# The order of TensorE's steps and of two copies in a fused attention with inverse-distance weights

## The reference, cut to what matters

```python
def _shepards_mha(Q, K, V):
    q2 = jnp.sum(Q * Q, axis=-1, keepdims=True)
    k2 = jnp.sum(K * K, axis=-1, keepdims=True)
    sq = q2 + jnp.swapaxes(k2, -1, -2) - 2.0 * jnp.einsum('bhqd,bhkd->bhqk', Q, K)
    dist = jnp.sqrt(jnp.maximum(sq, 0.0))
    W = (SHEP_EPS + dist) ** (-SHEP_P)                     # eps 1e-4, power 2
    W = W / (SHEP_EPS + jnp.sum(W, axis=-1, keepdims=True))
    return jnp.einsum('bhqk,bhkd->bhqd', W, V)

P = jnp.einsum('btd,ed->bte', Xn, W_in) + b_in             # Q, K, V and a gate G
A = _shepards_mha(Q, K, V)
return X + jnp.einsum('btd,ed->bte', G * A, W_out) + b_out
```

## Time and profile before

| | us |
|---|---|
| median of three executions | 3915.79 |
| the profiled execution | 3922.57 |
| its span | 3920.8 |
| PE busy in the span | 3543.4 (90%) |
| DVE busy | 2494.0 (64%) |
| ACT busy | 2228.7 (57%) |
| POOL busy | 646.5 (16%) |

### The profile page before, as it was taken

One profiled execution on the slowest core, in us unless ns is written; L12 is line 12 of the kernel. 1 busy time (PEld: TensorE's weight loads), 2 busy tenths in 40 slices (PEclk: granted clock), 3 DMA queues, 4 the chain that ended last, 5 costly groups with the idle time before them and its releaser, 6 DMA issues.

```text
span 3920.8 us, 56053 instructions
## 1 busy us (share of the span) xinstructions
PE 3543.4 (90%) x22244; PEld 2491.0 (64%) x22244; DVE 2494.0 (64%) x4347; ACT 2228.7 (57%) x2875; POOL 646.5 (16%) x595
## 2 busy tenths in 40 slices
PE   4999999989999999978779779779877999999998
PEld 3555555478888899973323323323326888889998
DVE  4777777553433455547988988988985443335554
ACT  1666666643322344438998998998993332234443
POOL 3333332100122011221300300200000002200212
PEclk7999999899999999988889889889888999999999
DMA  3000000010011134430000000000001001013342
GB/s 123 1 1 1 1 1 1 1 65 6 25 37 32 34 94 115 105 76 8 1 1 1 1 1 1 1 1 1 1 1 65 6 22 38 24 45 91 94 111 40
DMA packets 86664, 124.81 MB, mean 32 GB/s; under 512 B 7752, under 2 KB 73115, under 8 KB 86402
## 3 DMA queue, kind: packets, MB, share of 16 engines
q1 hardware_dynamic: 68738, 100.05, 7.5%
q0 software_dynamic: 17664, 21.17, 3.3%
HBM read 85.02 MB, written 42.55 MB: 33 GB/s over the span
## 4 chain that ended last, share of the span: by engine, by line
PE 32%; ACT 10%; DVE 9%; issue 3%; DVEq 1%; ACTq 0%; POOL 0%; DMA 0%; SPq 0%; POOLq 0%
PE f2ring L1479 14%; PE f2acc L1498 7%; DVE b_w L1831 6%; ACT b_w L1869 5%; PE b_acc L1946 4%; PE b_ring L1958 4%; ACT b_w L1909 4%; ACT L1906 1%; PE b_ring L2008 1%; DVEq L1770 0%; PE b_ring L2006 0%; DVE b_stacks L1747 0%; PE b_ring L1982 0%; PE f2ring L1444 0%; DVE b_w L1775 0%
## 5 line engine op out<-in xcount | busy, mean ns | idle before, releaser
L1831 DVE TENSOR_TENSOR b_w<-b_w 128x2048 f32<-128x2048 f32 x254 | 571.7, 2292 | 25.7 <-ACT b_w L1909 21.7
L1869 ACT ACTIVATE b_w<-b_ring 128x1024 f32<-128x1024 f32 x512 | 485.9, 1037 | 92.2 <-PE b_ring L1958 86.3
L1946 PE MATMUL b_acc<-b_w,b_vg 128*32 128x512 f32 x2048 | 333.0, 740 | 172.6 <-DVE b_w L1831 171.5
L1909 ACT ACTIVATE b_w<-b_w 128x2048 f32<-128x2048 f32 x256 | 468.7, 1897 | 2.1 <-issue 0.4
L1399 ACT ACTIVATE f2hid<-f2ring 128x512 f32<-128x512 f32 (+2 forms) x256 | 132.6, 518 | 577.4 <-PE f2ring L1479 560.4
L1399 ACT ACTIVATE f1hid<-f1ring 128x512 f32<-128x512 f32 (+2 forms) x256 | 132.6, 518 | 576.8 <-PE f1ring L1479 559.8
L1317 DVE TENSOR_TENSOR f1hid<-f1hid,f1ring 128x512 f32<-128x512 f32 (+2 forms) x256 | 150.2, 587 | 439.4 <-ACT f1hid L1399 439.4
L1317 DVE TENSOR_TENSOR f2hid<-f2hid,f2ring 128x512 f32<-128x512 f32 (+2 forms) x256 | 150.2, 587 | 439.3 <-ACT f2hid L1399 439.2
L1958 PE MATMUL b_ring<-b_qT,b_kT 32*128 32x512 f32 x2048 | 411.4, 692 | 18.6 <-ACT b_w L1869 15.0
L1775 DVE TENSOR_SCALAR b_w<-b_w 128x2048 f32<-128x2048 f32 x256 | 305.7, 1225 | 86.7 <-ACT b_w L1869 85.8
L624 ACT ACTIVATE a_prob<-a_wide 128x1024 f32<-128x1024 f32 (+1 forms) x320 | 292.8, 943 | 86.5 <-PE a_wide L730 59.6
(11 more groups left out here) (340 smaller groups left out, 6274.9 us busy)
## 6 DMA issues: line engine op xcount, KB each, us to landing
X<-expert_in SPq DMA_DIRECT2D x16, 650.0 KB, 4.8
expert_in<-a_zeros SPq DMA_DIRECT2D x8, 650.0 KB, 10.1
X<-in_x SPq DMA_DIRECT2D x4, 1024.0 KB, 10.7
x_mid<-X SPq DMA_DIRECT2D x8, 512.0 KB, 3.1
f1raw_x<-in_rd SPq DMA_DIRECT2D x4, 1024.0 KB, 5.3
f1raw_xf<-in_rg SPq DMA_DIRECT2D x4, 1024.0 KB, 5.0
f1raw_xf<-in_ru SPq DMA_DIRECT2D x4, 1024.0 KB, 7.1
f1raw_g<-in_rg SPq DMA_DIRECT2D x4, 1024.0 KB, 4.9
```

The costliest lines, as they stand in the source:

```text
L1831: v.tensor_tensor(one(m), one(m), one(m), ALU.mult).then_inc(s_wts, 1)
L1869: s.activation(w[:, m, 2 * pair:2 * pair + 2, :].rearrange("p h n -> p (h n)"), slot(at + pair), ACT.Ln, scale=SHEP_EPS ** -2).then_inc(R. ...
L1909: s.activation(one(m), one(m), ACT.Sigmoid, scale=-0.5).then_inc(s_sig, 1)
L1946: last = pe.matmul(acc[32 * h:32 * h + 32, qc, :], vg[:, u % 2, h, x, :], w[:, x, h, :], start=(x == 0), stop=(x == TB - 1))
```

## The change

TensorE's list. In the kernel before, between the `values` of period j stood one `dist` tile ahead of m=3, and one each ahead of m=5, 6 and 7; four followed after m=7. Now the tiles 0 and 1 stand back to back ahead of `values` m=3, one each ahead of m=4, 5, 6 and 7, and two follow after m=7. `stack` moves from the start of the odd period to the even period before it: the first stands ahead of `values` m=6, the second at the very end of the period. `project` no longer stands among the `values` m=0 to 2 but between the two `dist` tiles. VectorE's two copies move with their transposes: from after the squares m=0 and 1 of the odd period to after `bound` m=3 (behind `o_rows`) and m=7 of the even one. No instruction is added or removed.

```diff
@@ moved(j)
-        if j % 2 and (j + 1) // 2 < UNITS:
-            out += [("stack", (j + 1) // 2, i) for i in range(SIDES)]
@@ order(j)
+        stacks = [("stack", j // 2 + 1, i) for i in range(SIDES)] if j % 2 == 0 and j // 2 + 1 < UNITS else []
...
         for m in range(TB):
             if m == TB - 5:
-                out += aux + ahead[:1]
-                aux = []
-            elif m > TB - 4:
-                out += ahead[m - TB + 4:m - TB + 5]
-            elif m < TB - 5:
+                out += ahead[:1] + aux + ahead[1:2]
+            elif m > TB - 5:
+                out += ahead[m - 2:m - 1] + (stacks[:1] if m == TB - 2 else [])
+            elif aux and aux[0][0] != "project":
                 out += aux[:1]
                 aux = aux[1:]
             out += [("values", j, m)]
-        return out + ahead[4:]
+        return out + ahead[6:] + stacks[1:]
@@ VectorE, among the squares of period j
-                        elif m < SIDES:
-                            operand(n, m)
@@ VectorE, among the bounds of period j + 1, behind o_rows
+                    if j % 2 == 0 and n < UNITS and m in (3, TB - 1):
+                        operand(n, m // 4)
```

## The result

| | before | changed |
|---|---|---|
| median of four executions, us | 3916.45 | 4033.68 |
| lowest and highest | 3913.46, 3922.16 | 4030.2, 4038.35 |
| span of the profiled execution | 3920.8 | 4028.4 |
| granted clock over the span | 0.941 | 0.923 |

The ratio is 1.0298, with a 95% interval of 1.028 to 1.0316: 117 us slower, where 46 had been forecast and 3985 us was the end of the range. The direction is right. The places are right in part: the phases of p=0, which were to gain 2 us, lose 21. The loss is two and a half times as large.

The account below looks back on a forecast made before the run. ScalarE was taken to bound the second attention. Phase terms +17 (odd), +25 (plain even), +9.5 (p=4), +2.4 (period 30), -2.4 (p=0) and -5.7 (p=1) gave +46 on 3915.8: 3961.6 us, range 3925 to 3985.

Parts of the forecast that it names:

- p=0: Three phases with `project`: 6.39 us idle goes, second tile at T + 2 to T + 6; -2.4 us in all.
- ScalarE bounds the stage and only the logarithm phases can move: Second attention: ScalarE busy 1042.87 of 1136 us; the change can move only the logarithm phases, 556.0 us together.
- the clock's term: TensorE after T: half clock after a long wait makes odd phases 18.6 us instead of 16.4; even ones at full clock.
- Odd phases, the lone pair at half clock after the wait: Twelve odd phases: TensorE waits some 4 us, then runs at 1.2 GHz; 18.6 against 17.2 us, +17 in all.
- p=4: Three phases: half clock plus the stack's transposes and slot wait, 18.6 + 0.95 + 2.1 against 18.5; +9.5 us in all.
- Even phases: Nine plain even phases: full clock, plus stack transposes and slot wait, 19.5 against 16.7 us; +25 in all.
- The slot's chain: Even phases: after `values` 7, `o_rows` and the copy run before tile 6 with nothing beside them, 2.1 us.
- p=1: Three phases, without a stack: 16.9 to 18.9 against 19.5 us; -5.7 us in all.
- Period 30: One phase without a stack, priced at half clock: 18.6 against 16.2 us, +2.4.
- The rival of a full clock: TensorE stays at 2.4 GHz over the wait; odd, p=4 and period 30 phases 2.2 us shorter: +11, 3927; chance 0.14.
- the rival of half clock in even periods: Plain even phases: clock falls again in the wait or has not risen yet; 9 x 2.2 = +20, 3982; chance 0.13.

Follow-up runs that it names:

- e11: The changed kernel with its second distance tile computed whole and needless whole-array filler matmuls in the wait ahead of it (filler not at p=0 and 1): 3991.2 us, ratio 1.0189.
- e3: The kernel before with only `project` moved behind the first distance tile: 3912.3 us, ratio 0.9982.
- e4: The changed kernel with VectorE's copy into `b_qT` put one place ahead of `o_rows`: 3965.9 us, ratio 1.0112.
- e13: e11 with e4's exchange and fillers ahead of `values` 1 and 2 in even periods, `values` 0 in odd ones: 3935.3 us, ratio 1.0043.
- e5: The changed kernel with `project` put back among `values` 0 to 2: 4064.4 us, ratio 1.0377.
- e7: The kernel before with a needless lone pair of distances behind each of `values` 0, 1 and 2 of odd periods: 4009.3 us, ratio 1.0219.
- e12: The changed kernel with its second distance tile waiting until it can be issued whole, no filler: 4015.1 us, ratio 1.0234.
- e9: The kernel before with e3's place of `project` and needless whole-array filler matmuls ahead of `values` 0 to 2: 3900.4 us, ratio 0.9961.

## Why the prediction was right in direction and wrong in size

- *ScalarE bounds the stage and only the logarithm phases can move*: right. They grew by 114.8 us, and what lies between them did not move.
- **The step that failed is the clock's term.** It was mis-sized in the odd phases, put at nothing in the even ones, and at p=0 the place of the second tile behind `project` was forecast too early. The three follow.
- *Odd phases, the lone pair at half clock after the wait*: the mechanism is right, to the hundredth up to T + 4.95; e11 (16.9 without wait and pair) shows that the clock, and not the order, makes these phases long. The term's size is wrong: 18.6, "four more steps of 2.07, less what is still slow in the first (1.44 to the next `values`)", from the single row of p=4. Measured 19.6. Tile 3 starts at T + 8.35 and not at T + 7.4, tile 6 at T + 14.8 and not at T + 13.6, as the half clock holds for all of tile 2 and half of the `values` behind it. That is 12 us of the error.
- *Even phases*: 19.5 forecast, 22.3 measured. The slot's chain is right (1.95 against 2.1). I took the half clock as absent there, a rival at 0.13 and +20, and held that the first pair would end near T and no wait matter. From T + 1 to T + 4 the clock is 0.50 to 0.80 in six of nine, in four of them since it had not risen before T, which is one of the two ways that the rival named. And behind the pause of the slot the 1.2 GHz is back for tile 6 or 7 in 7 of 15, which no case of mine had, though it is the mechanism that I had used for the other end of the phase. Where the clock is full after T the phase is still 20.7; those three are all at p=2, where the phases of the kernel before were longer too (17.1 to 17.8, against 16.4), and what is left of the difference isn't resolved. 25 us; another 5 at p=4, where the same holds (23.4 against 21.65).
- *p=0*: -2.4 forecast, +21 measured. The place of the second tile, "T + 2 to T + 6 (as `project` runs at full or half clock)", was T + 9.5. `project` starts at T - 2.9 and takes 12.4 us at half clock. The trace of the kernel before had a hint: there it runs from 2091.84 to 2102.38, 10.5 us, the most part at half clock, and ScalarE's 6.39 us ahead of T stand behind it. That the clock would be at half through all of it was not to be read there, and what decides it stays open. The place itself is harmless: with `project` at full clock the phase is 18.9 in the old order (e3) and 19.2 in the new (e4, e13), less than the 23.2 of before. It is the second largest miss, 24 us.
- *p=1*: -5.7 forecast, -4.9 measured. Right; e5 shows that the gain belongs to the move of `project` (28.6 without).
- *Period 30*: 18.6 forecast, 19.8 measured, as the odd ones.
- *The rival of a full clock* (3927) is refuted by the 0.50 to 0.60 in 11 of 12 odd phases; *the rival of half clock in even periods* (3982) holds in part, and with the other misses is what carries the time out of the range. The range was too narrow because each of its ends varied one term, while the misses nearly all come from the clock and add up: 12 + 25 + 5 + 1 + 24 + 1 = 68, and 46 + 68 = 114.

## What to carry to other kernels

A TensorE that is waited for should come out of its waits at the full clock: before moving a step, look at the granted clock a few microseconds before and behind each wait, not only at the durations, and price a new pause with the slower matmuls behind it (here 1.9 us of pause cost up to 1.9 more). A matmul pair that used half of the rows cost as much time as a whole tile, and with such pairs in between the clock did not rise (e7), so issue all groups together where the ring has room. Waiting for room alone brought 19 us of the 117 (e12), with work in the wait 43 (e11). When a buffer is handed back by an engine that works in order, put the copy that frees it ahead of whatever waits for the same consumer: here exchanging two calls brought 68 us by the medians, some 32 of the 50 in the profiled execution by the pause itself.

## What was not expected of the hardware

- A lone pair of 32-row matmuls takes 2.08 us at 1.2 GHz, a tile of four 2.09; at 2.4 GHz 1.14 for the tile. Sixteen microseconds without a gap, with lone pairs among the first `values`, stayed at a granted clock of 0.51; with whole tiles at the same places the clock was up after the first.
- `project` (matmuls of one row for the bias and 128x128 ones) stayed at 0.50 for 12.4 us without a gap; behind it a whole `dist` tile at 2129.57 was still at half clock (2.09), and the next, 3.5 us later, at full. Started at 2.4 GHz it stayed there in e3, e4 and e13 and fell to half inside in the kernel before.
- The same steps with the same pauses (0.73 and 2.46 us) ended at half clock in one phase of e4 and at full in the next of its kind, 314 us later.
- Filler matmuls whose result nobody reads made a kernel faster: e9's bring the stage from 5085 to 5980 matmuls, the clock over the span goes from 0.941 to 0.975, and the time is 12 us below that of e3, which is the same kernel without them.
